# Two semaphore counters of a pipelined two-layer recurrence: who resets them, and how often

## The reference

```python
def layer(x, h0, Wx, Wh, b):
    xW = einsum('ntd,dh->nth', x, Wx) + b
    h = h0
    for t in range(T):            # T = 1024
        h = tanh(h @ Wh + xW[:, t])
        hs[:, t] = h
    return hs

x = x + layer(x, cond, Wx0, Wh0, b0)   # x is (8, 1024, 512)
x = x + layer(x, cond, Wx1, Wh1, b1)
```

## Time and profile before

| | us |
|---|---|
| median of 3 runs | 2182.45 (2181.98 to 2184.05) |
| the profiled execution's own time | 2181.98 |
| its span, first to last instruction | 2180.2 |
| PE busy | 2157.1 |
| DVE busy | 1306.2 |
| ACT busy | 807.7 |

### The profile page before, as it was taken

The page is one execution under the profiler, slowest core; times in us unless marked ns, Lnnn a source line. Parts: engine busy times, 40 slices in busy tenths (PEclk is TensorE's granted clock), DMA queues, the critical chain, the costliest instruction groups (busy, mean ns, idle before and its releaser), DMA issues.

```text
span 2180.2 us, 192439 instructions
## 1 busy us (share of the span) xinstructions
PE 2157.1 (99%) x90304; PEld 2127.9 (98%) x90304; DVE 1306.2 (60%) x5643; ACT 807.7 (37%) x3585; POOL 8.6 (0%) x11
## 2 busy tenths in 40 slices
PE   7999999999999999999999999999999999999997
PEld 7999999999999999999999999999999999999997
DVE  3566666666666666666666666666666666666665
ACT  2333333333333333333333333333333333333333
POOL 1000000000000000000000000000000000000000
PEclk9999999999999999999999999999999999999999
DMA  3000000000000000000000000000000000000000
GB/s 101 23 26 22 26 22 26 22 26 22 26 22 26 22 26 22 26 22 26 22 26 22 26 22 26 22 25 23 24 23 25 23 25 23 24 24 23 25 22 17
DMA packets 112033, 55.84 MB, mean 26 GB/s; under 512 B 12448, under 2 KB 111024, under 8 KB 111536
## 3 DMA queue, kind: packets, MB, share of 16 engines
q1 hardware_dynamic: 111456, 53.53, 8.5%
q10 hardware_dynamic: 432, 1.18, 0.1%
q0 software_dynamic: 32, 0.02, 0.0%
HBM read 37.90 MB, written 16.78 MB: 25 GB/s over the span
## 4 chain that ended last, share of the span: by engine, by line
PE 99%; DVE 0%; DMA 0%; issue 0%; ACT 0%; SPq 0%; DVEq 0%; ACTq 0%
PE ps L221 41%; PE ps_rec L238 21%; PE ps_rec L249 16%; PE ps L210 10%; PE ps_xw L210 10%; DMA wx<-wx_in 0%; DVE zt L391 0%; DVE z L397 0%; ACT h L331 0%; DVE zt L387 0%; ACT h L324 0%; SPq L180 0%; SPq L178 0%; DVE h L405 0%; DVEq L53 0%
## 5 line engine op out<-in xcount | busy, mean ns | idle before, releaser
L221 PE MATMUL ps<-wh,h 128*32 128x128 f32 x32768 | 1089.6, 273 | 4.9 <-ACT h L324 2.8
L221 PEld LDWEIGHTS ps<-wh,h 128*32 128x32 f32 x32768 | 907.9, 110 | 22.9 <-ACT h L324 5.1
L238 PE MATMUL ps_rec<-wh,h 128*32 128x128 f32 x16384 | 638.8, 273 | 7.8 <-ACT h L331 7.1
L391 DVE STREAM_TRANSPOSE zt<-ps_rec 128x128 f32<-128x128 f32 x1024 | 324.6, 317 | 423.2 <-PE ps_rec L249 417.0
L405 DVE TENSOR_TENSOR h<-h 128x16 f32<-128x16 f32 x2050 | 359.4, 175 | 354.4 <-ACT h L331 319.1
L249 PE MATMUL ps_rec<-wh_part,h 128*32 128x128 bf16 x24576 | 534.2, 219 | 0.9 <-issue 0.8
L324 ACT ACTIVATE h<-zt 128x32 f32<-128x32 f32 x1024 | 235.1, 230 | 725.1 <-DVE zt L387 725.1
L238 PEld LDWEIGHTS ps_rec<-wh,h 128*32 128x32 f32 x16384 | 463.1, 110 | 14.8 <-ACT h L331 13.4
L331 ACT ACTIVATE h<-z 128x32 f32<-128x32 f32 x1024 | 235.1, 230 | 637.4 <-DVE z L397 637.4
L249 PEld LDWEIGHTS ps_rec<-wh_part,h 128*32 128x32 bf16 x24576 | 460.2, 97 | 2.7 <-issue 1.6
L210 PE MATMUL ps<-wx,x_pe 128*32 128x128 f32 x8192 | 414.7, 273 | 4.8 <-ACT ps L306 3.0
(11 more groups left out here) (21 smaller groups left out, 22.7 us busy)
## 6 DMA issues: line engine op xcount, KB each, us to landing
x_pe<-x_t SPq DMA_DIRECT2D x256, 64.0 KB, 2.0
x_dve<-x_t SPq DMA_DIRECT2D x256, 64.0 KB, 2.0
out_t<-x_out SPq DMA_DIRECT2D x256, 64.0 KB, 1.5
wx<-wx_in SPq DMA_DIRECT2D x4, 256.0 KB, 8.0
wh<-wh_in ACTq DMA_DIRECT2D x1, 1024.0 KB, 8.6
wh<-wh_in SPq DMA_DIRECT2D x1, 1024.0 KB, 4.7
wx<-wx_in SPq DMA_DIRECT2D x1, 1024.0 KB, 8.2
bias<-b_in ACTq DMA_DIRECT2D x2, 64.0 KB, 4.0
```

What stands on the lines that cost most here:

```text
L221: mm = pe.matmul(rows(ps0[n // S4 % 2], g), h_step(0, n - 1)[:, k, :], wh[0][:, k, g * P:(g + 1) * P], start=False, stop=k == KC - 1, skip ...
L238: pe.matmul(rows(bank, g), h_step(1, n - 1)[:, k, :], wh[1][:, k, g * P:(g + 1) * P], start=False, stop=False, skip_group_check=True, tile ...
L391: dve.transpose(zt[1][n % 2][:, :], ps_rec1[n % 2][:, 0:P]).then_inc(zt1_done, 1)
```

## The change

`split_done` and `seed0_done` become one semaphore each. Their makers only add to them. PE, the only engine that waits for them, subtracts: once ahead of its loop (7 and 3), and at the end of each pass of the loop's body what that pass has waited for (8 and 2). Outside the loop its waits compare with the count less what has been taken off so far. `h_done` stays a pair that ACT resets.

```diff
-        seed0_done = [sem(f"seed0_done{j}") for j in range(2)]
+        seed0_done = sem("seed0_done")
...
-        split_done = [sem(f"split_done{j}") for j in range(2)]
+        split_done = sem("split_done")
...
         @block.tensor
...
+            split_base = seed_base = 0
...
-                    pe.wait_ge(*split_count(n - 1))
+                    pe.wait_ge(split_done, n - split_base)
...
-                        pe.wait_ge(seed0_done[c % 2], 1)
+                        pe.wait_ge(seed0_done, c - 1 - seed_base)
...
+            def taken(r):
+
+                return RING * r - 1 - LAG, 2 * r - 1
...
+            split_base, seed_base = taken(FIRST)
+            pe.sem_inc(split_done, -split_base)
+            pe.sem_inc(seed0_done, -seed_base)
             with pe.Fori(0, AFTER - FIRST, 1):
                 turn(FIRST)
+                pe.sem_inc(split_done, taken(FIRST)[0] - taken(FIRST + 1)[0])
+                pe.sem_inc(seed0_done, taken(FIRST)[1] - taken(FIRST + 1)[1])
+            split_base, seed_base = taken(AFTER)
...
         @block.scalar
...
-                        seed(0, c).then_inc(seed0_done[c % 2], 1)
-                    c = (n + 3) // S4
-                    if n % S4 == 1 and 2 <= c < NG:
-                        act.sem_inc(seed0_done[c % 2], -1)
+                        seed(0, c).then_inc(seed0_done, 1)
...
         @block.vector
...
-                rest(n, 2).then_inc(split_count(n)[0], 1)
+                rest(n, 2).then_inc(split_done, 1)
...
-                    if n % S4 == 0 and n:
-                        done, count = split_count(n - 1)
-                        dve.sem_inc(done, -count)
```

More of the change, by code:

```diff
@@ L132, in h_count @@
             return h_done[s // S4 % 2], steps.index((l, s)) + 1
-        def split_count(n):
-            s = n + LAG
-            return split_done[s // S4 % 2], s % S4 + 1
         block = ctx.enter_context(nc.Block())
```

## The result

The changed kernel takes 2219.13 us (median of 6 runs, 2218.80 to 2221.88) against 2182.22 us before in the same series (6 runs, 2181.24 to 2184.05): ratio 1.0171, 95% interval 1.0157 to 1.0183. It is slower, by 36.9 us. I had said 2209, with a range up to 2217: the direction was right, the size too small, the time outside the range.

A forecast was written before the change was run, and what follows sets the result against it. It took PE, at the loop body's end its sequencer, to bound the kernel. From the profiled 2181.98 us: + 29.0 (Part 1) + 0.2 (subtractions ahead of the loop) + 0 (Part 2) - 2.0 (Part 3) = 2209.2; range 2191 to 2217.

The forecast's parts named there:

- Part 1: End of PE's loop body: two semaphore instructions in each of 125 passes, 116 ns each, add 29.0 us.
- the draining rival: End of PE's loop body: an update waits until earlier matmuls are done, 0.79 us more a pass, 2279 us; chance 0.05.
- The upper bound of 208 ns a piece: Most that one new PE semaphore instruction could cost, the taken branch's length; 52 us for all.
- Part 2: DVE and ACT lose L440 and L346; costed at nothing, 9.7 us were all of it on the path.
- Part 3: DVE's 16 stalls between x_out and x_mid fall to about two: 3 us won, 2 us after giving 1 back.
- the 1 us given back for ACT: ACT goes from 18 to 17 instructions in four steps; its fetches may fall on new places, 1 us lost.
- Cheap: End of PE's loop body: the sequencer goes on at once after each subtraction, 51 ns each, 2193 us; chance 0.14.
- covered: End of PE's loop body: matmuls already handed over hide both subtractions, costing nothing, 2180 us; chance 0.08.

The follow-up runs named there:

- b_two_waits: Kernel before with two semaphore instructions that only wait, for semaphores long met, at the end of PE's loop body: 2210.37 us, ratio 1.0123.
- b_two_adds: Kernel before with two additions to semaphores nobody waits for, at the end of PE's loop body: 2222.94 us, ratio 1.0177.
- three_subs: Changed kernel with the 8 taken off split_done as 4 and 4, so three updates in a pass: 2241.46 us, ratio 1.0267 to before.
- mid_long: Changed kernel with the two subtractions moved to the middle of the second step, between a projection and recur1: 2181.65 us, ratio 0.9988 to before.
- mid_short: Changed kernel with the two subtractions moved to the end of the fourth step, no branch behind them: 2181.63 us, ratio 0.9989 to before.
- rot_mid: Changed kernel with PE's loop turned by half a step and the two subtractions in the middle of the fourth step: 2174.76 us, ratio 0.9959 to before.
- one_sub: Changed kernel with only split_done as one counter, seed0_done again a pair reset by ACT: 2200.48 us, ratio 1.0078 to before.
- b_shift4: Kernel before with four semaphore updates at the very start of DVE's stream: 2180.21 us, ratio 0.9984.

## Why the prediction was wrong in size, and where it was right

**That PE's sequencer at the end of the body bounds, and that anything more there is paid in full: right.** One, two and three updates lie on a line from the first on, and the same updates in the middle of the body cost nothing.

**Part 1, the price of a semaphore instruction, 51 + 65 = 116 ns: this is the step that failed.** From an update to the sequencer's next instruction it is 151 to 156 ns. 250 of them make 0.153 x 250 = 38.3 us instead of the 29.0 in the sum, and that 9.3 us is nearly the whole miss of 10.1. The 46 passes with 30 ns more, which nothing in my working could tell, add 1.4; the stalls gave 2.7 us instead of the 2.0 in the sum, 0.7 the other way. What I did wrong is exact: my nearest rows were an addition, and semaphore instructions that only wait. For those the price was nearly right (b_two_waits, 0.111 with its own 30 ns passes in it). The new instructions update, and the trace of before had no update by PE's sequencer among matmuls, as I had written myself under the draining rival. The Trainium skill's page Perfetto Trace Analysis, section Per-instruction lifecycle, puts the push of the update behind the reported window. The traces agree in this: the instruction that updates and the one that only waits are both 51 ns long, yet 0.153 and 0.108 us pass to the next one. I used that rule to add the 65 ns of an instruction that pushes nothing, and left the push itself unpriced. The runs put the difference between the two at 0.045 us; that this is the push alone was not shown.

**The range: wrong for the same reason.** The upper bound of 208 ns a piece held, but the range was cut at about 135 ns and so at 2217. With the far bound kept it would have reached 2232. An unseen operation priced from a neighbour of another kind deserved its far bound.

**Part 2, nothing won by taking L346 and L440 away: right.** In b_two_adds they stand and in the changed kernel not, and the passes differ by what the stalls explain: 17.05 against 17.03, where 13 long passes fewer, 0.21 us each, make 0.022 in the mean of 124.

**Part 3, DVE's stalls from 16 to about two: right**, two in the trace. Of the 1 us given back for ACT, 0.2 showed: the one new stall at 1144.6. All five kernels whose ACT has 17 instructions a group (the changed one, three_subs, mid_long, mid_short, rot_mid) have a longest wait of 0.7 us for ACT's tanh there, and the eight with 18 have 0.4; a second such wait, 0.66 at 50.6 us, lies ahead of the loop (the changed kernel's line, then one_sub's):

```profile
DVE h L408 <- ACT h L337: 318.6, 1024, 0.7
```

```profile
DVE h L409 <- ACT h L335: 319.3, 1024, 0.4
```

**The rivals.** Cheap (51 ns a piece) and covered were both refuted by the 17.01 of a pass; covered is what becomes true where the lead is longer, as mid_long shows. Draining was refuted by the first subtraction at 1004.4, ahead of loads still to come. Of what the profile was to show, the load gap at the body's end is 0.60, not 0.53, and a pass 17.01, not 16.94: both by the same 0.07. In the last pass, where the branch falls through, the gap is 0.50 and not 0.40; that pass is one of those with 30 ns more.

## What to carry to other kernels

On an engine that is busy all the time, ask of each sequencer instruction not how long it is but how far its sequencer is ahead at that place, and what stands there already: here two updates were free in the two places of a loop's body that were tried, and cost 1.7% behind the last matmul, next to the taken branch. A counter's reset is cheap where the sequencer is ahead, and so is the loop's branch; turning the loop by half a step won 0.3%. And a price for an instruction of a kind that the trace does not show wants its far bound in the range.

## What was not expected of the hardware

A semaphore instruction on PE's sequencer is 51 ns long in the trace whether it waits or updates, but 0.11 us pass to the sequencer's next instruction when it only waits and 0.15 when it updates. A weight load behind an update starts after 0.076 (mid_short). In 46 of 124 passes of the changed kernel one step of the sequencer was 30 ns longer: ahead of the second subtraction in one pass, of the addition in the next, of the branch in the one after, and mostly again eight passes later. three_subs has it in 109 of its 125, ahead of the addition or the branch. b_shift4, whose PE stream is that of before, shows such 30 ns ahead of its branch in 31 passes, every fourth, and the kernel before in none. What causes it stays open. And four idle semaphore instructions at the head of DVE's stream make the kernel 0.16% faster.
